# A gather and mixture-of-experts kernel: the next superblock's chain cut into sixteen segments around the experts' second products

## The reference

```
x = x + gnn(layernorm(x))          # two rounds of: rows gathered by edge, times weight, summed by dst, plus own row
x = x + moe(layernorm(x))
def gnn(f):  o = relu(batchnorm(S(f @ W1)));  return S(o @ W2)
def moe(t):                         # 8 experts, top 2
    logits = t @ router_w.T;  rw, re = top_k(softmax(logits), 2);  rw /= sum(rw)
    out = t
    for e in range(8):
        out += combine[:, e:e+1] * (gelu(t @ w1[e] + b1[e]) @ w2[e] + b2[e])
```

## Time and profile before

| | us |
|---|---|
| median of 3 runs | 4614.71 |
| the runs | 4610.76 to 4619.99 |
| time of the profiled execution | 4628.39 |
| its span | 4626.6 |

### The profile page before, as it was taken

One profiled execution on the slowest core, in us unless ns is written; L12 is line 12 of the kernel. 1 busy time (PEld: TensorE's weight loads), 2 busy tenths in 40 slices (PEclk: granted clock), 3 DMA queues, 4 the chain that ended last, 5 costly groups with the idle time before them and its releaser, 6 DMA issues.

```text
span 4626.6 us, 83922 instructions
## 1 busy us (share of the span) xinstructions
PE 3828.6 (83%) x26914; PEld 3346.5 (72%) x26914; DVE 3301.2 (71%) x8596; ACT 2957.3 (64%) x6463; POOL 2841.5 (61%) x2961
## 2 busy tenths in 40 slices
PE   1688888888789998965688888888888888888888
PEld 1688788778677777744577777777777777777778
DVE  8788888888688888855466666666666666666656
ACT  3688888889777777753455555555555555555555
POOL 0477777767566565646666666666666666666551
PEclk9999999999899999976798998988998989999989
DMA  8788888888799898963333333333333333333221
GB/s 237 278 315 309 310 316 308 304 316 293 272 308 305 296 315 292 311 189 116 93 98 101 107 100 98 106 98 99 108 101 102 106 100 108 102 102 106 79 82 30
DMA packets 308791, 857.91 MB, mean 185 GB/s; under 512 B 47937, under 2 KB 133018, under 8 KB 305852
## 3 DMA queue, kind: packets, MB, share of 16 engines
q0 software_dynamic: 140032, 442.58, 29.1%
q1 hardware_dynamic: 166148, 396.53, 26.8%
q10 hardware_dynamic: 2172, 13.35, 0.8%
HBM read 545.71 MB, written 306.56 MB: 184 GB/s over the span
## 4 chain that ended last, share of the span: by engine, by line
PE 54%; DVE 16%; issue 12%; ACT 8%; another core or an unknown queue 4%; DMA 4%; POOL 2%; SPq 0%; ACTq 0%; DVEq 0%; POOLq 0%
PE ps L1765 11%; PE ps L1744 10%; PE ps L1635 4%; PE ps L1464 3%; PE ps L893 2%; DVE S L1410 2%; PE ps L1639 2%; PE ps L1637 2%; PE ps L894 2%; PE ps L862 2%; DMA L<-msgd 2%; PE ps L851 2%; ACT A L959 2%; DVE low L1414 2%
## 5 line engine op out<-in xcount | busy, mean ns | idle before, releaser
L1550 POOL DMA_INDIRECT G<-h,tabT x1440 | 1461.7, 1015 | 828.8 <-issue 383.3
L1843 ACT ACTIVATE ps<-ps,b1T 128x500 f32<-128x500 f32 (+1 forms) x432 | 266.8, 618 | 780.4 <-remote 462.9
L959 ACT ACTIVATE A<-ps,A 128x256 f32<-128x256 f32 x1728 | 689.4, 510 | 83.1 <-PE ps L894 78.7
L1010 POOL DMA_INDIRECT msgd<-A,tabT x432 | 551.5, 1277 | 285.9 <-ACT A L959 169.8
L1616 ACT ACTIVATE gH<-G,tabT 128x256 fp32r<-128x256 f32 x960 | 449.0, 500 | 186.8 <-remote 64.1
L1994 DVE SCALAR_TENSOR_TENSOR X<-ps,X 125x256 f32<-125x256 f32 x800 | 347.0, 477 | 283.2 <-remote 239.5
L893 PE MATMUL ps<-winH,DT 128*128 128x256 f32 x1728 | 474.2, 306 | 51.8 <-issue 18.5
L1596 DVE SCALAR_TENSOR_TENSOR gL<-G,tabT,gH 128x256 fp32r<-128x256 f32 x960 | 442.3, 479 | 80.7 <-ACT gH L1616 52.8
L894 PE MATMUL ps<-winL,DT 128*128 128x256 f32 x1728 | 437.3, 285 | 0.0
L1637 PE MATMUL ps<-gH,s 128*125 128x256 f32 x1067 | 349.8, 329 | 63.1 <-issue 30.6
L893 PEld LDWEIGHTS ps<-winH,DT 128*128 128x128 f32 x1728 | 333.8, 193 | 60.6 <-issue 37.7
(11 more groups left out here) (333 smaller groups left out, 11094.8 us busy)
## 6 DMA issues: line engine op xcount, KB each, us to landing
L<-msgd SPq DMA_DIRECT2D x400, 520.0 KB, 5.6
A<-sbd SPq DMA_DIRECT2D x54, 861.0 KB
msgd<-A SPq DMA_DIRECT2D x100, 325.0 KB
G<-h,tabT POOLq DMA_INDIRECT x1440
winR<-h SPq DMA_DIRECT2D x108, 128.0 KB
A<-in_x SPq DMA_DIRECT2D x10, 1120.0 KB
h<-A ACTq DMA_DIRECT2D x10, 1120.0 KB
acc<-h SPq DMA_DIRECT2D x10, 1120.0 KB
```

Source lines behind the costliest of these rows:

```text
L959: e.activation(M[:, n, 0:F], psum[4 + v % 4][:, (n % 2) * F:(n % 2 + 1) * F], ACT.Identity, scale=M[:, n, F + 2:F + 3]).then_inc(evc, 1)
L1010: e.indirect_dma_start(msgd, bass.IndirectOffsetOnAxis(ap=idxI[g % 4][:, t:t + 1], axis=0), msg[g % 3][:, t * 4 * RW:(t + 1) * 4 * RW], No ...
L1550: e.indirect_dma_start(B.G[c % GRL], None, of, bass.IndirectOffsetOnAxis(ap=tab3[:, m, 0:1].bitcast(I32), axis=0)).then_inc(gatl[c % GRL], 16)
```

## The change

`moe_order` gives out two segments with each expert, one ahead of `down` as before and one behind it. `first` is cut to fit: on PE, ACT and DVE each step gets a segment of its own, so that a superblock of four blocks has sixteen and one of two blocks thirteen. The transposes and their copies go out by halves, the product with W2s and the statistics by pairs of blocks, the variance ends one segment and the reciprocal begins the next, the scaling to the normed rows goes out by halves, the logits by pairs, the routing in two parts, ACT's scaling of the output rows by pairs, the bias product and its add by pairs. Segment 7 is empty on PE behind the norm, and segment 13 behind the routing. No arithmetic changes. The ticks inside the chain stay eleven for a superblock of four, at most one to a segment. PE's single wait for the add of the bias (`d2_o2`) becomes one for each bank.

The segments on each engine, for four blocks:

| | PE | ACT | DVE |
|---|---|---|---|
| 1, 2 | transposes, two halves | their copies | tick in 2 |
| 3, 4 | W2s product by pairs | ticks | add and statistics; variance in 4 |
| 5, 6 | ticks | square root in 5 | reciprocal, scaling by halves |
| 8, 9 | transposes back | copies and high parts | rest parts |
| 10, 11 | logits by pairs | scaling of the output rows | copy to indices in 11 |
| 12 | tick | tanh | weights |
| 14 | transposes of weights | their copy | |
| 15, 16 | bias product by pairs | ticks | its add by pairs |

```diff
@@ moe_order
                 next(nxt, None)
                 down(i, ex, tick)
+                next(nxt, None)
@@ pe_last, first
-                if i:
-                    e.wait_ge(d2_o2, pairs_before(i))
                 for k in range(2):
+                    if k:
+                        yield
+                    if i:
+                        e.wait_ge(d2_o2, pairs_before(i) - 1 + k)
...
                     m.then_inc(d2_z, 1)
                     tick()
-                yield
-                tick()
-                tick()
+                    yield
+                for _ in range(2):
+                    tick()
+                    yield
                 yield
                 e.wait_ge(d2_t, i + 1)
                 for k in range(2):
+                    if k:
+                        yield
...
-                m.then_inc(d2_lg, 1)
+                    if j % 2:
+                        if j + 1 == n:
+                            m.then_inc(d2_lg, 1)
+                        tick()
+                        yield
                 tick()
-                tick()
-                tick()
+                yield
                 yield
                 e.wait_ge(rt_c, i + 1)
...
                     m.then_inc(d2_b2, 1)
                     tick()
+                    yield
@@ act_last, first
                 for h in range(0, n, 2):
                     tick()
-                yield
+                    yield
                 e.wait_ge(d2_v, i + 1)
                 e.activation(v[:, 12:12 + n], v[:, 8:8 + n], ACT.Sqrt).then_inc(d2_sq, 1)
-                tick()
-                tick()
+                for _ in range(2):
+                    tick()
+                    yield
                 yield
                 for k in range(2):
+                    if k:
+                        yield
                     e.wait_ge(d2_tt, 2 * i + k + 1)
...
+                tick()
+                yield
                 e.wait_ge(d2_k, 2 * (i + 1))
...
-                m.then_inc(d2_o, 1)
-                tick()
-                yield
+                    if j % 2:
+                        if j + 1 == n:
+                            m.then_inc(d2_o, 1)
+                        tick()
+                        yield
                 e.wait_ge(rt_s, i + 1)
                 e.activation(rt[:, 4:4 + n], rt[:, 0:n], ACT.Tanh, scale=0.5).then_inc(rt_e, 1)
                 tick()
-                tick()
-                tick()
+                yield
                 yield
@@ dve_last, first
+                yield
                 tick()
                 yield
...
                 for h in range(0, n, 2):
+                    if h:
+                        yield
                     e.wait_ge(d2_z, pairs_before(i) + h // 2 + 1)
                     e.tensor_tensor(X[:, h * F:(h + 2) * F], X[:, h * F:(h + 2) * F], bank(i, "z", h // 2)[0:R, :], ALU.add).then_inc(d2_x1, 1)
                     tick()
-                yield
-                e.wait_ge(d2_x1, pairs_before(i) + n // 2)
-                for j in range(n):
-                    own.done(e.bn_stats(stats[:, 6 * j:6 * j + 6], X[:, j * F:(j + 1) * F]))
+                    e.wait_ge(d2_x1, pairs_before(i) + h // 2 + 1)
+                    for j in range(h, h + 2):
+                        own.done(e.bn_stats(stats[:, 6 * j:6 * j + 6], X[:, j * F:(j + 1) * F]))
...
                 e.tensor_scalar(v[:, 8:8 + n], v3[:, 0:n, 1], EPS, None, ALU.add).then_inc(d2_v, 1)
+                yield
                 tick()
                 e.wait_ge(d2_sq, i + 1)
...
                 for j in range(n):
+                    if j == n // 2:
+                        yield
                     m = e.tensor_scalar(Zs[:, j * F:(j + 1) * F], X[:, j * F:(j + 1) * F], v[:, 2 * j:2 * j + 1], v[:, 16 + j:17 + j],
...
-                e.wait_ge(d2_tt, 2 * (i + 1))
-                e.wait_ge(d2_tc, 4 * (i + 1))
+                yield
                 if i >= 2:
                     e.wait_ge(l1s, 16 * (i - 1))
                 for k in range(2):
+                    if k:
+                        yield
+                    e.wait_ge(d2_tt, 2 * i + k + 1)
+                    e.wait_ge(d2_tc, 4 * i + 2 * k + 2)
...
+                if n > 2:
+                    yield
                 e.wait_ge(d2_lg, i + 1)
...
                     own.done(e.max_index(ix[:, 8 * j:8 * j + 8], m8[:, j, :], p8[:, j, :]))
                 tick()
+                yield
...
                 tick()
                 yield
                 yield
+                yield
                 e.wait_ge(d2_o, i + 1)
...
                     tick()
+                    yield
```

## The result

The changed kernel takes 4660.16 us (median of 6 runs, 4641.68 to 4669.79) against 4612.86 us for the kernel before in the same rounds: a ratio of 1.0093, 95% interval 1.0077 to 1.011. It is slower, by about 43 us, and lies above the predicted range. The profiled execution took 4656.12 us.

The account below looks back on a forecast made before the run. PE, busy 87% of the last stage, was taken as the bound. From the 4614.7 us median, 66 us off for removed waits and 8 added for two-block superblocks, net 58, gave 4557 us; range 4490 to 4650.

Parts of the forecast that it names:

- Removed waits: ACT's waits before square root and tanh, 2.06 + 3.95 = 6.0 us per superblock, should go nearly whole.
- What is that to PE?: In the last stage, half of ACT's removed 6.0 us reaches PE: 3.0 us in each of 22 superblocks, 66 us off.
- Handoffs that become shorter: Three PE-ACT(-DVE)-PE chains, cut to half an expert: tightest 3.1 us, covered by a 4.20 us `down`, so PE waits 0 us.
- Rival B: Shorter handoffs stall PE 1.5 us each, 99 us against 66 gained, plus 8: slower, 4656 us; chance 0.26.
- What moves: Bias product leaves the seventh expert and `d2_o` comes some two experts later, delaying SP's next `xt` load; costed at nothing.
- The load of x: SP's load of the next `xt` starts later, at no cost; if late, DVE's add of the z product would be late next.
- Two-block rounds: In four two-block superblocks `down` is too short a cover: 1 us at each of two handoffs, 8 us added.
- C: PE's losses are its own, ACT's waits only lay beside them: cutting the chain moves nothing, 4615 us; chance 0.14.
- D: All of ACT's 6.0 us per superblock come back and the clock holds: 4491 us; chance 0.12.
- A: The forecast itself: half of ACT's lost waits in the last stage reach PE, 4557 us; chance 0.48.

Follow-up runs that it names:

- hroot: Kernel before with only DVE's statistics and variance half an expert ahead of ACT's root: 0.9997 on a 4600-us chip.
- hybrid_2: Kernel before with variance and DVE's difference half an expert ahead of root and tanh, weights' transposes and bias product later: 1.0038 (4600-us chip); first run 0.9996 (4250-us).
- b16_2: Changed kernel with bias product and its add for both pairs in segment 16: 1.005 to kernel before (4600-us chip); first run 0.9973 (4250-us).
- short_l: Kernel before with only PE's logits half an expert nearer to the transposes back: 1.0036 on a 4250-us chip.
- short: Kernel before with PE's logits and bias product each half an expert nearer to what they wait for: 1.0056 on a 4600-us chip.
- wide: Changed kernel with all three shortened handoffs widened to a whole expert: to kernel before, 0.9962 on a 4250-us chip, 1.0048 on a 4600-us one.
- lg11: Changed kernel with all logits in segment 11: to kernel before, 0.9976 on a 4250-us chip, 1.0084 on a 4600-us one.
- before_again: Kernel before, unaltered, run again for its profile on a 4600-us chip: 4586.36 us.
- late: Kernel before with the weights' transposes, their copy, the bias product and its addition one expert later: 0.9995 on a 4250-us chip.

## Why the prediction was wrong, by its own steps

**Removed waits: right.** 6.0 us of ACT's idle time per superblock is 0.3.

**"What is that to PE?", 22 x 3.0 = 66 us off: the step that failed.** I took half of an engine's removed idle time as the bottleneck's gain, for want of a row. For the root, that half is 1.03 x 22 = 23 us; hroot has it alone and gives 0.9997, 1 us, at most 8 by its interval. Its rows say why: ACT is ahead of PE at these steps, and stands most of that time before its next copy instead. hybrid_2, with both waits gone (5.3 us left of some 120), is 17 us slower, not 66 faster; it also moves the weights and the bias product, so it is no clean test of the tanh's wait. The argument that PE's 8.0 idle us in those stretches were more than ACT's 6.0 showed only that both happen there.

**"Handoffs that become shorter", 0 us on paper: wrong too.** The three cost about 0.0034 of the time (1.0082 less 1.0048), 16 us or 0.7 per superblock, with an interval of about 0.003 either side, and b16_2 returns as much alone. Shortened in the kernel before, the logits' cost 15 us and the bias' 8, but short_l loses it wholly and short for the larger part behind the 20 superblocks; a price per superblock of four blocks does not follow from them. My 3.1 us counted the instructions of the handoff and one gelu with its high part ahead of it. Missing were what else stands ahead of them on ACT in order (a chunk that waits for its gather, a table load of 1.28 us), and on 4600-us chips how late PE's result arrives: 7.2 us in the timeline of after.

**Rival B** had this mechanism, and its 4656 us is close to the 4660 measured. That is mostly luck: it had 99 us of stalls less 66 gained, and the runs show 16 and none.

**What moves, costed at nothing: open.** The changed kernel's loss of 0.0082 to 0.0096 leaves 0.0048 (22 us) when the handoffs are wide. hybrid_2 has 0.0038 without any of the cuts into halves, and hroot none. The rest of the loss may therefore be what hybrid_2 has and hroot has not: the tanh one place later, or the weights and the bias product an expert or more later, on a 4600-us chip. That the two figures are alike does not show that they have one cause, and the cutting into halves was never taken alone. On a 4250-us chip it seems to pay: wide, lg11 and b16 are at 0.9962 to 0.9976 where hybrid is at 0.9996. The load of x, which I had as the first thing to come late, did not: DVE's idle time before the add of the z product is 49.6 us in the stretch of before and 38.5 in that of after.

**Two-block rounds, 8 us:** small, as thought. The last four rounds' periods (first L1684 or L1687 of each) sum to 249.9 us before and 253.2 after; on the chip of before_again the whole end takes 304.4 us before and 301.9 after. In short and short_l, where the cover is a two-block `down`, it was not small: 18 us each.

**C** (PE's losses are its own) was right on what the root's removed wait is worth, and wrong that nothing else moves. **D** fell with A.

No version tried beats the kernel before on a 4600-us chip; on a 4250-us one wide does, by 0.4%.

## What to carry to other kernels

Idle time in front of an engine that runs ahead of the bottleneck is slack. Before you count its removal as a gain, follow the engine to the next thing that it takes from the bottleneck: if it will stand there, the gain is nothing. Measure a handoff not by its own instructions but from the producer's last one to the consumer's first, with all that stands ahead in order on each engine between, at its slowest; if that is longer than the cover, the bottleneck waits there. Even then a wait with a name is not yet a loss, as it can take the place of another: compare the length of the same stretch in both kernels, part by part. Here 78.8 us of new waits left 20 superblocks no longer than without them, and the whole loss, 13 to 18 us, lay behind them.

## What the runs showed of the hardware

Chips differ by 8% on the same kernel: 4252 and 4253 us on two, 4582 to 4616 us on three more and in the runs of the result. Take the 20 superblocks of late on a 4250-us chip and of before_again on a 4600-us one, shown above (the two kernels hold the same work, and late takes the time of before on its chip). 230 us lie here: PE is busy 127 us less, at a granted clock of 0.97 in place of 0.91, and idle 123.7 us in place of 226.9. DVE's and POOL's times are alike. On the 4600-us chips PE's waits bear "issue" and ACT's "remote", and PE's results reach ACT up to 7 us after the record of their end; on the others the same waits name the instruction that PE waits for, and ACT's idle before the copy of the transposes back is 0.0 us in the 20 superblocks of all seven kernels profiled there. Why was not found. The sign of a small change can hang on it: wide is 0.9962 on one kind and 1.0048 on the other.
